# First q kept on chip, the weight-scale chain ahead of the constant tables, later loads behind the q pieces, and a new order of all engines' steps

## What is computed

```python
xn = _layernorm(x)                       # x: (8, 256, 512)
# layer 0 attention
qkv = xn @ Wqkv                          # q: 32 heads x 16; one k, one v
scores = jnp.einsum('bqhd,bkd->bhqk', q, k) * scale
scores = jnp.where(causal, scores + alibi, NEG_INF)
probs = jax.nn.softmax(scores, axis=-1)
attn = jnp.einsum('bhqk,bkd->bqhd', probs, v).reshape(B, S, H) @ Wo
# layer 0 ffn: top-2 gates over 4 experts of rank 16
delta = jnp.sum(gates[:, :, None] * jnp.einsum('ter,eor->teo', mid, B) * SCALE, axis=1)
x = x + attn + delta
xn = _layernorm(x)
# layer 1: per-token attention, and
h = jax.nn.silu(gate(xn)) * up(xn)       # 512 -> 1792, int weights with scales
x = x + attn1(xn) + down(h)              # 1792 -> 512
```

## Time and profile before

| | |
|---|---|
| runs | 623.84, 624.21, 625.64 us (median 624.21) |
| profiled execution, first to last instruction | 623.2 us |
| TensorE busy | 570.7 us (92%) |
| VectorE busy | 461.3 us (74%) |
| ScalarE busy | 377.0 us (61%) |
| GpSimd busy | 351.7 us (56%) |
| mean granted clock of TensorE | 0.959 |
| DMA | 34.97 MB, 98942 packets, 75548 of them under 512 B |

### The profile page before, as it was taken

One profiled execution on the slowest core, in us unless ns is written; L12 is line 12 of the kernel. 1 busy time (PEld: TensorE's weight loads), 2 busy tenths in 40 slices (PEclk: granted clock), 3 DMA queues, 4 the chain that ended last, 5 costly groups with the idle time before them and its releaser, 6 DMA issues.

```text
span 623.2 us, 14286 instructions
## 1 busy us (share of the span) xinstructions
PE 570.7 (92%) x5590; PEld 421.3 (68%) x5590; DVE 461.3 (74%) x1034; ACT 377.0 (61%) x703; POOL 351.7 (56%) x364
## 2 busy tenths in 40 slices
PE   4579583699999999999999999999999999999997
PEld 4466451467885668776968587858685876785783
DVE  4769874899999874899697748996986569354642
ACT  3287095847875478675757485858684776651240
POOL 6231595724655667674837574848576677542140
PEclk9987895599999999999999999999999999999999
DMA  8767799905054146001610160016001000000000
GB/s 207 152 95 78 123 237 217 170 2 54 2 54 87 37 68 70 3 4 35 88 17 5 35 86 4 4 35 88 1 5 52 18 1 9 28 2 2 35 1 34
DMA packets 98942, 34.97 MB, mean 56 GB/s; under 512 B 75548, under 2 KB 90044, under 8 KB 98876
## 3 DMA queue, kind: packets, MB, share of 16 engines
q1 hardware_dynamic: 76044, 24.58, 22.7%
q0 software_dynamic: 2352, 7.18, 5.7%
q10 hardware_dynamic: 20480, 2.31, 2.6%
HBM read 30.19 MB, written 8.39 MB: 62 GB/s over the span
## 4 chain that ended last, share of the span: by engine, by line
PE 68%; DVE 13%; SPq 8%; ACT 4%; issue 3%; DMA 2%; POOL 2%; ACTq 1%; DVEq 0%
PE B_bank L1266 27%; PE B_bank L1287 14%; PE A_bank L1218 7%; SPq L693 5%; PE A_bank L1191 4%; DVE mx L1537 4%; PE A_bank L1120 3%; PE E_bank L1176 3%; PE B_bank L1154 3%; PE E_bank L1171 2%; PE B_bank L1254 1%; DMA qq<-nmp 1%; ACTq L693 1%; SPq L731 1%; SPq L717 1%
## 5 line engine op out<-in xcount | busy, mean ns | idle before, releaser
L883 POOL TENSOR_TENSOR probs<-e,probs 128x512 f16<-128x512 f32 x176 | 208.3, 1188 | 127.2 <-ACT probs L999 126.8
L1266 PE MATMUL B_bank<-xs,wgu 128*128 128x256 f16 x1792 | 204.3, 273 | 0.3 <-DVE hf L1649 0.3
L998 ACT ACTIVATE e<-E_bank,wn 128x512 f32<-128x512 f32 x192 | 133.7, 696 | 103.4 <-PE E_bank L1176 53.9
L1266 PEld LDWEIGHTS B_bank<-xs,wgu 128*128 128x128 f16 x1792 | 172.7, 98 | 21.6 <-DVE hf L1649 0.6
L999 ACT ACTIVATE probs<-E_bank,wn 128x512 f16<-128x512 f32 x192 | 134.0, 698 | 0.0
L1287 PE MATMUL B_bank<-wd,hbuf 128*128 128x512 f16 x448 | 99.9, 379 | 0.1
L897 POOL TENSOR_TENSOR hbuf<-hf,hbuf 128x512 f16<-128x512 f32 x56 | 65.8, 1176 | 56.2 <-ACT hbuf L1033 55.8
L1537 DVE TENSOR_REDUCE mx<-B_bank 128x2 f32<-128x384 f32 (+5 forms) x168 | 92.1, 603 | 4.5 <-PE B_bank L1154 4.4
L1639 DVE SCALAR_TENSOR_TENSOR hf<-ebuf,B_bank 128x512 f32<-128x512 f32 x56 | 38.3, 684 | 62.2 <-ACT ebuf L1043 61.9
L1287 PEld LDWEIGHTS B_bank<-wd,hbuf 128*128 128x128 f16 x448 | 43.2, 98 | 49.3 <-POOL hbuf L897 0.6
L1043 ACT ACTIVATE ebuf<-B_bank,sgx 128x256 f32<-128x256 f32 x112 | 47.5, 485 | 22.1 <-PE B_bank L1266 20.8
(11 more groups left out here) (199 smaller groups left out, 696.3 us busy)
## 6 DMA issues: line engine op xcount, KB each, us to landing
qq<-q_parts SPq DMA_DIRECT2D x21, 256.0 KB
x<-in_x SPq DMA_DIRECT2D x20, 256.0 KB, 3.1
out_y<-x SPq DMA_DIRECT2D x16, 256.0 KB, 2.0
xa<-in_x SPq DMA_DIRECT2D x12, 256.0 KB, 5.1
q_parts<-qs SPq DMA_DIRECT2D x48, 64.0 KB, 2.9
wgu<-in_gate_w POOLq DMA_DIRECT2D x4, 448.0 KB, 9.1
wgu<-in_up_w POOLq DMA_DIRECT2D x4, 448.0 KB, 8.7
wd<-in_down_w POOLq DMA_DIRECT2D x4, 448.0 KB, 7.1
```

Source lines behind the costliest of these rows:

```text
L883: pool.tensor_tensor(probs[:, u % PSLOTS, 1, :], e32[:, w, :], probs[:, u % PSLOTS, 0, :], ALU.subtract).then_inc(s_lop, 1)
L998: act.activation(e32[:, w, :], psum("exp", i, g, w)[:, :], ACT.Exp, scale=wn[:, 7:8])
L1266: mm = pe.matmul(psum(name, u, i)[:, a * SEQ:(a + 1) * SEQ].rearrange("p (t n) -> p t n", t=NU), wgu[:, m, k, (2 * i + a) * P:(2 * i + a + ...
```

## The change

It has five parts.

1. **First q on chip.** `store`, `gather_first` and the gather of sequence 1 go, and so do the DMAs that put alibi and zero rows into `qq` for the first two sequences. In their place each of the eight pieces of chunk 0's q (`b`, `m`: eight heads of one sequence) goes by three DMAs from SBUF to SBUF into a staging tile `natural[m]` with features on the partitions (SP, `place`), and one DVE copy takes all 64 rows, alibi and zero rows among them, into `qq` (DVE, `place`). `zero` clears the staging rows, SP's `tables` puts the alibi rows into the four staging tiles (eight DMAs). SP's `place` stands behind SP's `tables`.
2. **Maxima of sequence 0 without DMA.** `max` of sequence 0 goes in 32 groups, piece by piece. Its maxima are turned in two halves (`nm0`), and TensorE adds them in each `exp` step of that sequence: four more matmuls of 128 columns, with a column of `pick` as weights.
3. **Scale chain first.** The casts of the alibi tables move from DVE to ScalarE (`tables`), the mask work becomes a step of its own (`masks`), `identh` and `hot` are made from the fp32 identity; the order puts `norm` and `scale` ahead. ScalarE loads its exponential table by an exponential of one column at the end of `start`.
4. **Loads.** The constants are loaded between x tiles 1 and 2. x of chunk 1 follows the pieces of sequence 0, `wo` the pieces of sequence 1; `ffn_load` starts behind the last piece, and its last four (down weights) wait for the gather of sequence 3 and are waited for by `half`, no longer by `gate`. `hi`/`lo` split the token weights first (`HI_ORDER`).
5. **Order.** `US` and `RANK` are new for all steps of all engines (not shown: tables of numbers).

```diff
+FIRST_MAXG = [(tb, 2 * n, 2) for n in range(NK) for tb in range(NTB)]
+HI_ORDER = [NK, 0, 1, 2, 3] + list(range(NK + 1, 2 * NK + 2))
...
-        first = [sp("gather", i, gap=8.0) if i else sp("gather_first", NK - 1, gap=4.5), act("kT", i)]
+        if i == 0 and n % NTB == 0:
+            first += [dve("place", 0, n // NTB)]
+        if i == 1 and n == 0:
+            first += [dve("place", 1, NK - 1)]
...
-        p.add("ACT", ("store", b, m), dve("q0", b, m))
+        p.add("SP", ("place", b, m), dve("q0", b, m), *([] if b else [sp("tables", gap=0.0)]), *([dve("place", 0, m)] if b else []))
+        p.add("DVE", ("place", b, m), sp("place", b, m, gap=2.5))
...
             def tables():
-                sp.wait_ge(s_init, 4)
-                for b in range(NB):
-                    zero_rows(b, R_NM, R_HOT).then_inc(s_zero, 16)
+                sp.wait_ge(s_zero, NK)
                 sp.wait_ge(s_pos, 1)
-                for r0, rows in ((R_ALIBI, slope_up), (R_ALIBI + 3, pos_half)):
-                    for b in range(NB):
-                        sp.dma_start(qq[r0:r0 + 3, b, :, :, :].rearrange("a c h t -> a c (h t)"), rows).then_inc(s_posq, 16)
+                for m in range(NK):
+                    for r0, rows in ((R_ALIBI, slope_up), (R_ALIBI + 3, pos_half)):
+                        sp.dma_start(natural[m][r0:r0 + 3, :], rows[m:3 * NK:NK, :]).then_inc(s_natural[m], 16)
...
+            def place(b, m):
+                if b:
+                    sp.wait_ge(s_placed, m + 1)
+                for g, part in enumerate(PART_Q):
+                    if part == 0:
+                        sp.wait_ge(s_q0h, b * NK + m + 1)
+                    else:
+                        wait_used(sp, "q0", b, m)
+                    sp.dma_start(natural[m][g * HD:(g + 1) * HD, :].rearrange("d (h t) -> d h t", t=SEQ),
+                                 q_first[:, b, m, part, :]).then_inc(s_natural[m], 16)
...
             def ffn_load(n):
                 k = n // 2
                 if n == 0:
-                    pool.wait_ge(s_gather[1], 16 * 3)
+                    pool.wait_ge(s_natural[NK - 1], 32 + 48 * NB)
+                if n == 2 * NK:
+                    pool.wait_ge(s_gather[1], 16 * 4)
...
+            def tables():
+                act.wait_ge(s_rows, 32)
+                act.activation(pos_half, pos_nat, ACT.Copy)
+                act.activation(slope_up, slope_nat, ACT.Copy, scale=POS).then_inc(s_pos, 1)
...
+            def nm0(b, h):
+                wait_full(act, "nm0", b, h)
+                act.activation(nm_first[0:NG // 2, h, :], psum("nm0", b, h)[0:NG // 2, 0:P], ACT.Copy, scale=-1.0 / NM).then_inc(s_nm0, 1)
...
+                    for c1 in range(0 if i else blocks):
+                        row = g // 2 % 2 * 2 * NTB + 2 * (t0 + c1) + g % 2
+                        mm = pe.matmul(acc[:, c0 + c1, :, :], pick[:, row:row + 1].broadcast_to([NG, P]),
+                                       nm_first[:, g // (NHG // 2), :].rearrange("r (h t) -> r h t", t=GT), start=False, stop=True,
+                                       skip_group_check=True)
...
             def half(u, t):
+                if u == 0 and t == 0:
+                    pe.wait_ge(s_wd, 16 * (N_FFN - 2 * NK))
...
+            def place(b, m):
+                dve.wait_ge(s_natural[m], 32 + 48 * (b + 1))
+                dve.tensor_copy(qq[0:R_HOT, b, :, 8 * m:8 * m + 8, :],
+                                natural[m][0:R_HOT, :].rearrange("d (h c t) -> d c h t", c=NTB, t=GT)).then_inc(s_placed, 1)
```

372 lines of the change are left out of this document (198 added, 174 removed), and 20 rows, old and new, of tables (RANK, US).

## The result

The changed kernel is slower by 0.8%: 630.72 us as the median of 6 runs (628.73 to 631.11) against 624.92 (623.50 to 626.80) for the kernel before on the same chip. The ratio is 1.0078, 95% interval 1.0059 to 1.0098. The prediction was 602 with a range of 590 to 617: wrong in sign, and some 29 us off. The profiled execution spans 628.9 us, and its mean granted clock is 0.961 (0.959 before).

A forecast was written before the change was run, and what follows sets the result against it. TensorE's work plus its idle time was taken as the bound, with only the start able to give much. Idle −23.5, added matmuls +7 and clock −6 took the 623.2 us span to 600.7; plus 1.0 for the median, 602, range 590 to 617.

The forecast's parts named there:

- The first link: Start, sequence 0: first maximum at 29 us instead of 49.2, exponentials from 43 instead of 77.8.
- worth 4: Scale chain at the start: scale ready at 18.8 us in place of 22.8, 4 us on the chain, bounds 2 and 5.
- Done at about 36: TensorE's fp32 work for chunk 0 done at about 36 us, with 1.5 us of idle in place of 12.7.
- ready by 54: Second half of sequence 0's maxima: due 14 us after the exponentials start at 43, ready by 54.
- from 43 on ScalarE leads: Sequence 0's exponentials, paced by ScalarE, end at 79 us; the feed-forward part can start at 92 to 95.
- Rival 1: VectorE becomes the bound of the start and half of the 23.5 us is lost: 614 us, chance 0.20.
- Idle of 29: TensorE's idle over the whole span: 29 us against 52.5, a gain of 23.5.
- Added matmuls, +7: TensorE, sequence 0: 96 matmuls adding the maxima cost 7 us, bounds 5 and 12, all counted as work.
- Clock, −6: Middle stages of the start: a denser TensorE keeps two thirds of 17 us lost to low clock, 6 us gained.
- Rival 3: No shorter: TensorE waits as long further on, later gathers holding up sequence 2's maxima; 624 us, chance 0.04.
- Rival 2: Slower: down weights load late and the first `half` step waits for them; 621 to 628 us, chance 0.07.
- three signs: Wrong if: first exponentials after 55 us, a wait at `half` for `wd`, or over 6 us idle behind 130.

The follow-up runs named there:

- c_order_noreduce: Changed kernel with a model-searched order of the first 160 us and GpSimd's reduction across partitions replaced by a plain copy: 628.46 us, ratio 1.0046.
- a_rows: Changed kernel with the max rows of sequence 1 issued on SyncE ahead of the gather of sequence 2: 626.68 us, ratio 1.0013.
- d_order: Changed kernel with start orders searched again, reckoning with GpSimd's 13 us reduction and 2.6 us of SyncE per q store step: 628.13 us, ratio 1.0019.
- e_twice: Changed kernel with VectorE making every maxima reduction of sequence 1 twice: 639.13 us, ratio 1.0211.
- experiment 7: Idle matmuls put into TensorE's waits to raise its clock: 49 in d_order, 627.24 us (1.0023); 72 in a_rows, 625.93 us (0.9998).
- a_loads: Changed kernel with the feed-forward loads no longer waiting for the last q piece, issued from 49.1 us instead of 69.6: 631.6 us, ratio 1.0088.
- d_before: Kernel before, its instructions kept, with orders from the same search as d_order: 632.04 us, ratio 1.0089.
- the searched orders: Orders of the five engines up to some 160 us, found by search on a model: d_order 628.13 us, a second one 627.65, d_before 632.04.

## Why the prediction was wrong

**The first link was right.** First maximum 30.6 for 29, first exponentials 44.7 for 43, no wait for rows of sequence 0. The parts behind it were less so: the power of the scale chain is at 19.7, not near 17, and the scale is ready at 21.8, not 18.8. GpSimd's queue shows why: layer-norm steps and two DMA issues stand ahead of it.

```profile
17.41 0.82 POOL L874 DMA_DIRECT2D sg<-in_gate_s  x1
18.24 0.56 POOL L874 DMA_DIRECT2D su<-in_up_s  x1
...
19.15 0.57 POOL L892 TENSOR_TENSOR rs<-rs,mhalf 128x1 f32<-128x1 f32 x1
19.70 0.64 POOL L835 TENSOR_TENSOR wn<-wn,mhalf 128x1 f32<-128x1 f32 x1
```

So "worth 4" was 1 us. It did little harm by some luck: in the forecast the first piece had to wait for the alibi tables until 23.5 anyway, and it was issued at 23.2. The placement behind it went as forecast.

**"Done at about 36" and "ready by 54" failed.** Both took the work that was possible for the work that the order gives. `q0(1,3)`, the last fp32 piece, is at 61.7 and the second turn at 79.8, since steps of sequence 1 and chunk 1 stand between. Behind that, "from 43 on ScalarE leads" held only for the first twelve steps. The end of sequence 0's exponentials was forecast for 79 and came at 115.6. The late turn alone doesn't account for it: with it 10 us earlier, `c_order_noreduce` is at 112.2.

**The forecast didn't fit its own estimate for VectorE.** Rival 1 puts about 90 us of VectorE work between 14 us and the first feed-forward step. 14 + 90 is 104, later than the 92 to 95 of the forecast even if VectorE never waited. Measured, VectorE is busy 84.2 us from 14 to the end of sequence 0's exponentials (77.6 in the kernel before, which gets there at the same time), and 119.3 us from 14 to the first feed-forward matmul; some of that belongs to later sequences.

**The later links weren't in the sum.** I read the chain of before up to its first exponentials and let everything behind it move along. But the rows of sequence 1 hang on SyncE's queue, and that queue on chunk 1's q: its stores occupy it from 91.7 to 113.9 (71.4 to 105.2 before). The chain of waits of the changed kernel, from `q0(1,3)` on:

```profile
61.77 3.40 PE A_bank L1145 x8
...
83.07 1.34 PE A_bank L1152 x6
...
92.77 5.78 SPq L727
...
112.57 3.99 DMA q_parts<-qs
...
118.97 1.48 SPq L798
120.49 8.44 DMA qq<-nmp
128.98 0.62 PE E_bank L1214 x2
```

`a_rows` shows that the place of the last three of these lines costs 4.0 us. That the rest of it sets the end is what the chain says; no run shortened it in a way that paid.

**The step that failed** is the one from the first exponentials to the full part ("from 43 on ScalarE leads", feed-forward at 92 to 95, only local waits left), which the sum took in as 29 us of idle time. In its place the runs show that the head start of 33 us is used up by the end of sequence 0's exponentials (115.6 for 115.2 before), that the rows of sequence 1 then leave SyncE's queue 10.7 us later than before, 4.0 us of the time by their place in it, and that TensorE's idle time is 46.9 us and its first feed-forward matmul at 161.3. What between 45 and 115 us uses the head start up is not shown by a run; VectorE's work is the candidate that `d_order` and `e_twice` leave standing.

The span was to fall by 22.5 us and grew by 5.7. Of these 28 us, 17.9 are idle time (46.9 for 29) and 10.4 busy time (11.4 more in place of 7 − 6 = 1).

**Idle of 29 in place of 46.9.** Up to 6.84 us 6.8 (7), then 9.1 (1.5), 6.8 (3.5), 17.2 (10), 2.7 (3), and 4.1 at the end (4); in brackets the forecast. The first matmul comes at 7.95, 1.1 us later than before. The waits of TensorE name the largest parts behind it:

```profile
PE E_bank L1214 <- DMA qq<-nmp: 7.6, 1, 7.6
PE E_bank L1214 <- ACT probs L1027: 6.9, 5, 4.8
PE B_bank L1186 <- DVE wd L1512: 4.4, 1, 4.4
```

Of the three waits of the earlier trace rows the one for rows grew from 5.5 to 7.6, the one behind low probabilities fell from 7.2 to 2.5, and the 5.9 behind turned x are gone. In their place stand waits behind exponentials (the longest 4.8) and 4.4 us among the first maxima, until 35.3, while VectorE makes the table copies of sequence 1 and the second placement (29.2 to 34.4).

**Added matmuls, +7.** Mis-sized twice: 13.1 us busy, since one of them takes 0.14 us here (13.1 by 96) in place of 0.076, and 1.2 to 1.3 us of time. The prediction said that part is hidden and counted all. TensorE's busy and idle time mislead: they add up to the span, but a change of one term moves the other.

**Clock, −6.** The granted clock of the first 150 us is 0.84 for 0.83; no gain, and in the two stages where experiment 7 raised it, a higher clock was worth nothing that can be measured. The term presumed that TensorE is the bound in those stages.

**The rivals.** Rival 3 (the waits come back further on, through stores and later gathers) came nearest, at 0.04, and I put it at 624; with a better place for one entry it is 626.7. It named the maxima of sequence 2 as what is held up and the weight loads as the cause; the rows of sequence 1 were held up, and `a_loads` rules out the loads. Rival 1 (VectorE) is not ruled out: VectorE is near its limit and added work on it shows, but its price, half of the gain, was too low, as nothing of the gain was left. Rival 2 didn't happen: there is no wait for the down weights. My slower case was another mechanism than the one that came. Nor did any of the three signs show that were to mean "wrong": the exponentials start before 55, there is no wait at `half`, and the idle time behind 130 is 2.7 us. They watched the first link and the full part, and the loss lies between. The sign that did speak is the idle time up to 130: 5.4 us less, in place of about 20.

**What stays open.** What placing q on chip is worth by itself isn't known: `d_order` is 3.9 us shorter than `d_before`, but that search served the kernel before badly. No order was found that brings the changed kernel below the kernel before. Nor is it settled what holds the changed kernel between 47 and 115 us: single moves there didn't show, and no run took work from VectorE without giving it to another busy engine.

## What to carry to other kernels

A gain at the head of a chain counts only if each later link moves as well: follow every queue, SyncE's among them, down to the start of the full part, in the new order and not in the order that would be possible. Price added work on a waiting engine by what leaving it out gives, not by its busy time, and take no credit for a higher clock where that engine isn't the bound. Add up the work of each engine that the chain passes, VectorE's here, and see that it fits into the time that the forecast leaves. When two kernels differ in structure and in order, the order must be judged too: an order made in the same way for both helps only if it is no worse than the ones they came with.

## What was not expected of the hardware

**Reduction across partitions on GpSimd.** The trace shows 0.38 us of work and 13 us in which GpSimd does nothing else (in the changed kernel 5.6 ahead and 7.4 behind, in the kernel before 5.9 and 7.0). It cost 5.1 us of time where exponentials lie around it and nothing measurable elsewhere.

**VectorE beside GpSimd.** In the changed kernel, VectorE's small steps and then GpSimd's of the same moments:

```profile
48.88 1.17 DVE L1538 TENSOR_TENSOR rest<-lm 128x64 f32<-128x64 f32 x1
...
51.20 1.08 DVE L1543 TENSOR_TENSOR osum<-osum,rest 128x64 f32<-128x64 f32 x1
```
```profile
49.94 2.27 POOL L907 TENSOR_TENSOR probs<-e,probs 128x512 f16<-128x512 f32 x2
```

The last of them in the kernel before, where GpSimd stood still behind its reduction:

```profile
57.33 0.23 DVE L1485 TENSOR_TENSOR osum<-osum,rest 128x64 f32<-128x64 f32 x1
```

This step of 64 elements takes 1.08 us in place of 0.23, the one at 48.88 takes 1.17, and about 1.14 is what one GpSimd step of 512 elements takes (2.27 for two): VectorE waits for it. The same with a placement's copy: 1.65 us at 32.74 beside a GpSimd step, 0.68 alone. The prediction cited the Trainium skill (SBUF — State Buffer, section "SBUF: two separate sides") for the other direction; the rule there, that whichever of the two starts holds the shared ports until its instruction is done, agrees with these rows, and it names VectorE's operations with two inputs in SBUF, as this one has, among those that it holds for, beside a GpSimd operation that reads SBUF, as `probs<-e,probs` does.

**Issues on SyncE.** Eight q stores held its queue 12.6 us in one place and 7.3 in another; in the kernel before four took 23.7 us and four more 6.0. It is single issues that are long: of the sixteen in the changed kernel the median took 0.59 us and the longest 5.8, and of sixteen in the kernel before the median took 0.59 and the longest 15.3. What held those wasn't tested. With 2.6 us a step reckoned for them, the searched orders still came 5.7 us and more above their forecast.
